# Moving sixteen small on-chip transfers of a fused layer from ScalarE's DMA queue to the sync engine's

## The reference, cut to what matters

```python
c_kv = x @ W_dkv.T
q_lat = einsum('bqhd,hdl->bhql', (x @ W_dq.T @ W_uq.T).reshape(B, T, 16, 8), k_eff)
attn = einsum('bhql,bkl->bhqk', q_lat, c_kv) / sqrt(8)
attn = softmax(where(causal, attn, -inf), axis=-1)       # needs the maximum of each row
y_lat = einsum('bhqk,bkl->bhql', attn, c_kv)
```

## The kernel before, in words

| entries in order | near unit |
|---|---|
| `place_max` of batch 0, half 0 | before unit 0, among feed-forward tiles |
| `place_max` 0, half 1; then `qk` and `qk_rest` of batch 2 | 5 to 8 |
| `place_max` 1, half 0 | 13 |
| `place_max` 1, half 1 | 21 |
| `qk` and `qk_rest` of batch 3; then `place_max` 2, half 0 | 26 to 28; 29 |
| `place_max` 2, half 1 | 37 |
| `place_max` 3, half 0; half 1 | 45; 53 |

## Time and profile before

### The profile page before, as it was taken

One profiled execution on the slowest core, in us unless ns is written; L12 is line 12 of the kernel. 1 busy time (PEld: TensorE's weight loads), 2 busy tenths in 40 slices (PEclk: granted clock), 3 DMA queues, 4 the chain that ended last, 5 costly groups with the idle time before them and its releaser, 6 DMA issues.

```text
span 706.5 us, 11037 instructions
## 1 busy us (share of the span) xinstructions
PE 567.1 (80%) x3428; PEld 360.0 (51%) x3447; DVE 488.4 (69%) x1296; ACT 388.9 (55%) x618; POOL 329.1 (47%) x287
## 2 busy tenths in 40 slices
PE   3959789686776766598999899947789989988787
PEld 1413333243242222397989799923545545545466
DVE  4749999967989998535423655387677778887052
ACT  2666656575654454265766557524266556565741
POOL 5259989916986799222778323432012103112010
PEclk9979999987968998999999999966999999999999
DMA  5855555514676355200132201323103003000001
GB/s 140 300 162 145 154 178 158 155 42 143 204 248 202 111 162 139 78 28 16 52 108 69 80 17 42 98 82 89 28 3 105 10 2 108 3 3 1 2 16 46
DMA packets 50524, 65.92 MB, mean 93 GB/s; under 512 B 7730, under 2 KB 29250, under 8 KB 50210
## 3 DMA queue, kind: packets, MB, share of 16 engines
q1 hardware_dynamic: 45122, 59.27, 28.5%
q0 software_dynamic: 2496, 5.15, 2.0%
q10 hardware_dynamic: 2848, 0.78, 0.5%
HBM read 47.46 MB, written 9.52 MB: 81 GB/s over the span
## 4 chain that ended last, share of the span: by engine, by line
PE 32%; DVE 9%; issue 8%; POOL 5%; ACT 4%; ACTq 1%; DMA 0%; POOLq 0%; another core or an unknown queue 0%; DVEq 0%
PE ps L1621 30%; DVE arena L1541 3%; POOL moe_out L836 2%; ACT arena L1141 2%; POOL moe_rows L828 1%; PE ps L1917 1%; DVE x L1476 1%; DVE nb L1240 1%; DVE stats L1227 1%; POOL arena L881 1%; PE ps L1924 1%; ACT arena L1161 1%; ACTq L1131 1%; POOL arena L877 0%; ACT r L1141 0%
## 5 line engine op out<-in xcount | busy, mean ns | idle before, releaser
L1621 PE MATMUL ps<-arena 128*128 128x128 f32 (+10 forms) x2131 | 328.6, 331 | 51.3 <-DVE arena L1541 18.0
L1621 PEld LDWEIGHTS ps<-arena 128*128 128x128 f32 (+2 forms) x2150 | 210.4, 160 | 136.4 <-issue 56.6
L1621 PE MATMUL ps<-arena,ident 128*128 128x512 f32 x256 | 134.8, 669 | 52.1 <-DVE arena L1423 52.1
L1411 DVE TENSOR_TENSOR_SCAN arena<-ps,arena 128x512 f32<-128x512 f32 x128 | 149.3, 1208 | 14.8 <-ACT ps L1067 6.8
L1067 ACT ACTIVATE ps<-arena 128x512 f32<-128x512 f32 x128 | 87.3, 690 | 84.5 <-DVE arena L1411 79.6
L1541 DVE CUSTOM_DVE_ANT_0 arena<-ps,cmask 128x128 f32<-128x128 f32 (+3 forms) x256 | 111.5, 487 | 26.8 <-PE ps L1621 25.4
L851 POOL TENSOR_TENSOR arena<-arena 128x1024 f32<-128x1024 f32 x64 | 126.8, 2000 | 1.5 <-DVE arena L1411 1.0
L1621 PEld LDWEIGHTS ps<-arena,ident 128*128 128x128 f32 x256 | 51.3, 211 | 131.4 <-DVE arena L1423 78.5
L836 POOL DMA_INDIRECT moe_out<-arena,xT x46 | 44.8, 973 | 70.1 <-DVE arena L1565 57.5
L1141 ACT ACTIVATE arena<-ps 128x1024 f32<-128x1024 f32 (+3 forms) x86 | 57.1, 709 | 36.0 <-PE ps L1621 35.6
L1595 DVE TENSOR_TENSOR arena<-arena,ps 128x512 f32<-128x512 f32 x46 | 31.7, 688 | 64.4 <-PE ps L1621 46.9
(11 more groups left out here) (199 smaller groups left out, 621.4 us busy)
## 6 DMA issues: line engine op xcount, KB each, us to landing
arena<-bc_rows SPq DMA_DIRECT2D x128, 256.0 KB, 3.8
arena<-arena SPq DMA_DIRECT2D x64, 64.0 KB
arena<-arena SPq DMA_DIRECT2D x28, 128.0 KB, 2.5
moe_rows<-arena SPq DMA_DIRECT2D x2, 1495.0 KB, 11.9
arena<-moe_rows SPq DMA_DIRECT2D x8, 325.0 KB, 4.9
arena<-in_L_attn_a_Wg SPq DMA_DIRECT2D x8, 256.0 KB, 3.9
arena<-in_L_attn_a_Wu SPq DMA_DIRECT2D x8, 256.0 KB, 5.1
arena<-moe_out SPq DMA_DIRECT2D x4, 512.0 KB, 5.2
```

The costliest lines, as they stand in the source:

```text
L1411: V.tensor_tensor_scan(hst[:, g % STATES, e, :], bank(6 + e), dBx[:, g % RING, e, :], 0.0, ALU.mult, ALU.add).then_inc(s_scan, 1)
L1621: return T.matmul(o, l, rr, start=start, stop=stop)
```

## The change

The two transfers of each `place_max` are issued by the sync engine instead of ScalarE. ScalarE still copies the rows to `mrow`; its wait for its own copy goes away with the transfers. The sync engine gets an entry `place_max`, in which it waits for that copy and issues the two transfers. The order of `steps`, and everything that waits for the transfers, stays as it was.

```diff
+            def place_max(b, q):
+                sp.wait_ge(s_mr, 2 * b + q + 1)
+                for r in range(2):
+                    sp.dma_start(qq[64 * r + QR:64 * r + QR + 24:8, b % SL, HP * q:HP * q + HP, :],
+                                 mrow[3 * HP * r:3 * HP * (r + 1), q, :]).then_inc(s_mp[b][q], 16)
+
             place_ones(0)
...
-            parts = dict(qk=place_first, qk_rest=place_rest)
+            parts = dict(qk=place_first, qk_rest=place_rest, place_max=place_max)
...
                 S.copy(mrow[0:6 * HP, q, :], max_rows).then_inc(s_mr, 1)
-                act.wait_ge(s_mr, n + 1)
-                for r in range(2):
-                    act.dma_start(qq[64 * r + QR:64 * r + QR + 24:8, b % SL, HP * q:HP * q + HP, :],
-                                  mrow[3 * HP * r:3 * HP * (r + 1), q, :]).then_inc(s_mp[b][q], 16)
```

## The result

The changed kernel takes 727.06 us (median of 5 runs, 724.08 to 730.95) against 719.96 us (5 runs). The ratio is 1.0108 with a 95% interval of 1.0074 to 1.0142: slower by 7.1 us by the medians and 7.8 by the ratio. The forecast was 725.3, in a range of 720.0 to 728.2.

The account below looks back on a forecast made before the run. TensorE was taken to set the pace in the attention, busy 88 to 89%. Stall +5.4, clock +1.7, time coming back -0.4 and ScalarE's gains -1.4 gave +5.3 us: 719.96 to 725.3 us, range 720.0 to 728.2.

Parts of the forecast that it names:

- The eighth place collides: At batch 2 half 0 the pair waits behind batch 3's 21 transfers on the sync engine, issued 7.5 us later.
- the stall: TensorE waits for the late pair before unit 32: 5.4 us lost, bounds 5.1 and 5.8.
- The clock: After TensorE's idling before unit 32, a stretch at 1.2 GHz costs 1.7 us, bounds 0 and 2.9.
- What comes back: The first unit after TensorE's idling runs without its usual waits: 0.4 us regained, between 0 and 2.0.
- stall mostly made up: Rival: full clock after unit 32's wait and six units without waits, +2.0 us, 722.0 us; chance 0.22.
- ScalarE's gains: Time freed on ScalarE at the places of place_max saves TensorE 1.4 us, bounds 0.5 and 3.7.
- The last place: At units 54 and 55 TensorE no longer waits for ScalarE's exponentials: 0.5 us gained.
- The four middle places: Batch 1 both halves, batch 2 half 1, batch 3 half 0: 0.2 us gained each, 0.8 in all.
- What the sync engine does late: Batch 2's query train starts half a microsecond late, place_ones and place_zeros come later; other work covers it, no cost.
- the first place: At the first place_max, around 499 us, VectorE could begin the maxima slightly earlier: 0.1 us gained.
- ScalarE's time counts in full: Rival: 1.6 us at each of seven places reaches TensorE, 11.2 in all; -5.8 us, 714.2 us; chance 0.06.
- Only issue time moves: Rival: moving issues saves only sequencer time and batch 2 half 0 costs nothing; 718.6 us; chance 0.06.

Follow-up runs that it names:

- e1_seven: The changed kernel, but the pair of batch 2 half 0 stays on ScalarE's queue; 718.09 us, ratio 0.9965 to the kernel before.
- e2_eighth: The kernel before, with only the pair of batch 2 half 0 moved to the sync engine; 727.03 us, ratio 1.0091 to the kernel before.
- e3_order: The changed kernel, with the batch 2 half 0 pair ahead of batch 3's 14 key transfers on the sync engine; 718.78 us, ratio 0.9970 to the kernel before.
- e5_half: The changed kernel, with the batch 2 half 0 pair issued after four of batch 3's last eight key transfers; 723.86 us in a single execution.
- e8_four_more: The changed kernel, with four more 64 KB transfers issued by the sync engine ahead of the batch 2 half 0 pair; 731.42 us in a single execution.
- e4_filler: The changed kernel, with 26 matmuls added on TensorE before its wait for the batch 2 half 0 pair; 724.49 us, ratio 1.0065 to the kernel before.
- e7_pool: The kernel before, with all eight pairs issued on GpSimd's queue instead of ScalarE's; 719.73 us, ratio 0.9991 to the kernel before.

## Why the prediction was right, point by point

**The place of the loss: right.** "The eighth place collides" was the step on which all hung, and it is shown from three sides: the loss moves with that one pair (e1_seven, e2_eighth), vanishes with its place in the sync engine's order (e3_order), and grows by 0.62 to 0.645 us with each issue ahead of it (e5_half, e8_four_more).

**Its size: 5.4 forecast, 5.9 measured.** In the changed kernel TensorE starts the scores at 612.64. The kernel before, moved by the 11.65 us that part the two traces from unit 2 to unit 31, started them at 595.14 + 11.65 = 606.79. So the stall was mis-sized by 0.45 us, and 5.86 lies just above the upper bound of 5.8. The pair is issued at 609.88 where 598.05 + 11.65 = 609.70 were due, and 0.38 us pass from the last data to TensorE's start where I had put 0.1 for the semaphore. The 14 key transfers were quicker without ScalarE's interference, as expected: 8.96 us instead of 9.21. But the seven query transfers ahead of them took 5.65 us in this execution instead of 5.24, so that the whole train took 14.7 us and not 14.3 as in e1_seven and e4_filler.

**The clock: 1.7 forecast, 2.1 measured.** The granted clock fell to 0.50 in the stall, at 611.82, for 6.8 us. The kind is right; that the size is near is in part luck. The 1.7 was half of a stretch of 3.4 us. What came was the long one, with 6.0 us of it on work, which by the same reckoning costs 3.0; it cost 2.1, and no run shows where the other 0.9 went. Nor is the term a constant. It was 1.1 in e2_eighth, and nothing in e5_half, whose idle stretch of 3.20 us was followed by full speed. The two stretches of the earlier trace rows would have let one expect a fall after 3.06 us.

**What comes back: 0.4 forecast, nothing measured.** In e5_half, where the clock did not fall, unit 33 is as late as the scores of unit 32, 3.37 us: the first unit behind the stall gained nothing. From unit 33 to 53 the changed kernel takes 50.55 us and the kernel before 50.56. VectorE was busy for 2.22 of the 5.68 us of the stall, and that shortened nothing afterwards. The case "stall mostly made up", which rested on this, falls with it.

**ScalarE's gains: 1.4 forecast, 0.6 measured.** The last place gave 0.54 (0.5 forecast), the first 0.06 (0.1 forecast; 1.26 instead of 1.32 us between the maxima on both sides of it). The four middle places were forecast at 0.2 each and gave 0.00. Their second halves do come early, by 0.21, 0.17, 0.48 and 0.21 us in units 15, 23, 39 and 47, but each time the next unit stands where it stood. The step that failed is the comparison of the earlier trace rows with the earlier trace rows. The 0.17 us was there, but the instruction to which I measured was not the one that sets the pace. Behind it stands a product for the maxima that waits for VectorE, and VectorE's turn had been started by TensorE's own product behind the value products, not by ScalarE. That is read from the traces; no run took VectorE's work away to show it.

**What the sync engine does late: right.** Its query train of batch 2 began at 543.33 where 531.02 + 11.65 = 542.67 would have been due, 0.7 us late (half a microsecond forecast), and no unit behind it moved.

**The sum.** +5.9 + 2.1 - 0.6 = +7.4, against 7.1 in the medians; the 7.2 of the trace lacks the first place and has the 0.2 us of units 0 to 2, which are not the change's. The forecast of +5.3 was low by 2.1 us because all four terms erred the same way: 0.5 in the stall, 0.4 in the clock, 0.4 in what comes back and 0.8 in ScalarE's gains. The measured 727.06 lies near the upper end of the range of 720.0 to 728.2.

**One step was wrong and did no harm.** I took 13.5 us to lie around the span, by setting a profiled span against a median of other executions. It is 1.8 us; the rest was the luck of that execution, in a stretch that the change does not touch.

**Rivals.** "ScalarE's time counts in full" is excluded by e1_seven: seven pairs taken off ScalarE gave 0.6 us, not 11.2. "Only issue time moves" describes e1_seven, e3_order and e7_pool, and would have been right, with gains of 0.6 instead of 1.4, had the sync engine been free at the eighth place.

## What to carry to other kernels

Moving transfers to an engine that is idle on average says nothing; look up, place by place, what stands ahead of each in that engine's program, and multiply the issues by their duration. Here seven of eight were free and one cost seven microseconds. Another order on the receiving queue, for that one pair, cures it. Before time freed on an engine is counted as gain, follow the next two waits of the engine that sets the pace: twelve microseconds freed on ScalarE gave 0.6, though the chain of waits ran through its issues at both ends. And compare stages that both traces have in common, not spans: the stage here repeats to 0.03 us while whole executions of the kernel before scatter by 6 to 8 (715.96 to 722.37 in 13 of them, 715.88 to 724.01 in 28).

## What the runs showed of the hardware that was not expected

- An idle TensorE of 3.20 us (e5_half) kept its clock of 2.4 GHz, while 3.06 us before 396.73 had been followed by 1.2 GHz; idle stretches of 5.26, 5.68 and 8.26 us all fell to 1.2 GHz before TensorE restarted. A half-speed stretch cost 1.1 us where 3.10 us of it lay on work, and 2.1 where 5.93 and 6.01 did.
- Issuing a pair of 12 KB transfers takes 1.47 us on ScalarE, 1.44 to 1.63 on the sync engine and 1.11 to 1.26 on GpSimd.
- Between the last data of a transfer and the start of the TensorE instruction that waits for it 0.38 us pass (last data at 612.26 in the changed kernel, start at 612.64).
